# Two layer norms centred by a product into a free bank, token transposes in a second bank, block counting in three pieces, side work at other steps

## The reference, cut to what matters

```python
x = x + gnn0(layernorm(x), adj, ...)                 # stage 1
x = x + experts0(layernorm(x)[None], ...)[0]         # stage 2, 8 experts, top 2
x = x + gnn1(layernorm(x), adj, adj, ...)            # stage 3: signed graph attention, 3 heads, and two GRU cells
x = x + experts1(layernorm(x)[None], ...)[0]         # stage 4

def layernorm(x, eps=1e-5):
    return (x - mean(x)) / sqrt(var(x) + eps)

# stage 4
logits = flat @ router_w.T
probs = softmax(logits)
topk_probs, topk_idx = top_k(probs, 2)
topk_probs = topk_probs / (sum(topk_probs) + 1e-9)
h = silu(flat @ w1[e]) * (flat @ w3[e])              # 8 experts, 341 hidden
out = sum over the two experts of gate * (h @ w2[e])
```

## Time and profile before

| | |
|---|---|
| median of three executions | 514.84 us |
| the profiled execution | 515.35 us |
| its span, first to last instruction | 513.5 us |
| mean granted TensorE clock | 0.946 of full |
| TensorE busy | 439.7 us (86%) |
| VectorE busy | 337.6 us (66%) |
| ScalarE busy | 233.6 us (45%) |
| GpSimd busy | 63.6 us (12%) |
| chain that ended last | PE 47%, DVE 26%, ACT 10%, issue 10%, POOL 3%, DMA 2% |

### The profile page before, as it was taken

The page is one execution under the profiler, slowest core; times in us unless marked ns, Lnnn a source line. Parts: engine busy times, 40 slices in busy tenths (PEclk is TensorE's granted clock), DMA queues, the critical chain, the costliest instruction groups (busy, mean ns, idle before and its releaser), DMA issues.

```text
span 513.5 us, 6127 instructions
## 1 busy us (share of the span) xinstructions
PE 439.7 (86%) x1754; PEld 255.0 (50%) x1756; DVE 337.6 (66%) x731; ACT 233.6 (45%) x377; POOL 63.6 (12%) x112
## 2 busy tenths in 40 slices
PE   4578597978799998998979998999987878889996
PEld 2533353544455664454644343444434446666886
DVE  0997979787637684224574789596766726774573
ACT  4988779586777651204034222222222114743431
POOL 5000000000010000000000000100320321264433
PEclk9579788998979999989999999999999989999999
DMA  8989300000000100000000000170100012013132
GB/s 287 301 253 400 138 0 0 0 1 1 0 3 0 54 2 0 1 0 2 0 2 0 1 0 31 50 235 26 37 22 1 22 47 57 28 34 89 59 107 80
DMA packets 25355, 30.44 MB, mean 59 GB/s; under 512 B 3266, under 2 KB 19855, under 8 KB 25319
## 3 DMA queue, kind: packets, MB, share of 16 engines
q1 hardware_dynamic: 22711, 26.56, 16.0%
q0 software_dynamic: 1568, 2.92, 1.7%
q10 hardware_dynamic: 1040, 0.52, 0.4%
HBM read 19.73 MB, written 10.26 MB: 58 GB/s over the span
## 4 chain that ended last, share of the span: by engine, by line
PE 47%; DVE 26%; ACT 10%; issue 10%; POOL 3%; DMA 2%; SPq 0%; DVEq 0%; POOLq 0%; ACTq 0%
PE bank L1344 8%; PE bank L1162 5%; DVE pr_ring L2120 3%; PE bank L1123 3%; PE bank L1421 3%; PE bank L1405 3%; PE bank L1292 2%; PE bank L1406 2%; DVE y_units L1546 2%; POOL xg L586 2%; DVE y_units L1557 2%; PE bank L1012 2%; PE bank L1333 2%; DVE t_units L1552 2%; DVE hr_ring L1921 2%
## 5 line engine op out<-in xcount | busy, mean ns | idle before, releaser
L1344 PE MATMUL bank<-pr_ring,hW 128*128 128x512 f32 (+3 forms) x198 | 94.5, 562 | 8.2 <-DVE pr_ring L2120 7.3
L2120 DVE SCALAR_TENSOR_TENSOR pr_ring<-adjT,regR,bank 128x512 f32<-128x512 f32 (+3 forms) x99 | 64.3, 680 | 34.4 <-PE bank L1333 33.2
L1344 PEld LDWEIGHTS bank<-pr_ring,hW 128*128 128x128 f32 (+1 forms) x198 | 34.3, 193 | 39.7 <-DVE pr_ring L2120 23.2
L1012 PE MATMUL bank<-y_units,msg 128*128 128x512 f32 (+3 forms) x66 | 34.4, 653 | 14.5 <-DVE y_units L1567 14.5
L1123 PE MATMUL bank<-hr_ring,W2s 128*128 128x512 f32 (+1 forms) x96 | 46.3, 571 | 0.0
L1921 DVE TENSOR_TENSOR hr_ring<-hr_ring,bank 128x512 f32<-128x512 f32 (+1 forms) x48 | 29.5, 621 | 22.5 <-ACT hr_ring L808 16.0
L808 ACT ACTIVATE hr_ring<-bank,b1c 128x512 f32<-128x512 f32 (+1 forms) x48 | 29.7, 628 | 15.5 <-PE bank L985 15.5
L983 PE MATMUL bank<-zhi,W1hi 128*128 128x512 f32 (+1 forms) x48 | 35.8, 747 | 0.3 <-DVE zlo L1541 0.3
L586 POOL DMA_INDIRECT xg<-rowx,slot x22 | 22.1, 1005 | 72.2 <-DVE slot L1678 62.6
L2161 DVE TENSOR_TENSOR hbuf<-hbuf,bank 128x341 f32<-128x341 f32 x30 | 15.3, 508 | 19.9 <-PE bank L1406 17.6
L1012 PEld LDWEIGHTS bank<-y_units,msg 128*128 128x128 f32 (+1 forms) x66 | 14.0, 224 | 27.8 <-DVE y_units L1567 18.3
(11 more groups left out here) (350 smaller groups left out, 871.2 us busy)
## 6 DMA issues: line engine op xcount, KB each, us to landing
xg<-zeros SPq DMA_DIRECT2D x1, 6110.0 KB
wall<-in_w SPq DMA_DIRECT2D x2, 1364.0 KB
adjT<-in_adjT SPq DMA_DIRECT2D x1, 2560.0 KB
xblk<-xg SPq DMA_DIRECT2D x30, 65.0 KB, 1.8
adjT<-in_adjT SPq DMA_DIRECT2D x1, 1650.0 KB
adjT<-in_adjT SPq DMA_DIRECT2D x3, 512.0 KB, 5.7
adjT<-in_adjT SPq DMA_DIRECT2D x1, 1024.0 KB
W1f<-in_W SPq DMA_DIRECT2D x1, 1024.0 KB, 11.6
```

Of the source, the lines that this page charges most:

```text
L1012: mm = nc.tensor.matmul(B_GNN[:, 0:w], msg[0:r, j, :], y_units[0:r, g % RINGY, i, 0:w], start=(j == 0), stop=(j == T - 1))
L1344: nc.tensor.matmul(B_ACC[:, 0:w], hW[0:r, j, k * P:(k + 1) * P], ring[0:r, 0:w], start=(k == 0 and j == 0), stop=(k == K - 1 and j == T - ...
L2120: nc.vector.scalar_tensor_tensor(out=pr_ring[0:r, 4 + p % R_RING, 0:w], in0=adjT[0:r, j, cols(c)], scalar=g_col[0:r, j, k:k + 1], in1=B_F[ ...
```

## The change

The norms of stage 4's chunks 0 and 1 are centred in another way. `mean` becomes a product of cmat (the unit matrix less 1/128) with xT, which gives x less its mean directly, into bk[2], one of the GRU cells' banks. ScalarE squares it from that bank, the first instruction of `scale` reads it there, and VectorE's `center` (line 1520) is gone for these two. The token transposes of chunks 0 and 1 go to bk[1] instead of B_SIDE, and the later gates products that use bk[1] wait for the copy. `starts` is cut in three pieces of 5, 5 and 3 instructions. Some entries of the tables move to other steps. The same number of instructions remains, but for the two centerings.

```diff
 MAIN_PE = {
-    (1, 10): [("mid", 0, 2)], (2, 1): [("turned", 3)], (2, 9): [("turned", 4)], ...
-    (3, 10): [("turned", 6)], (4, 0): [("turned", 7)], (4, 4): [("turned", 8), ("mean", 3, 0)], (4, 7): [("var", 3, 0)], (4, 10): [("logits", 3)],
-    (5, 1): [("ztok", 0)], (5, 3): [("prefix", 0)], (6, 0): [("gates", 1, 1)], (6, 2): [("mid", 1, 1)], (6, 8): [("mean", 3, 1)],
-    (7, 0): [("var", 3, 1)], (7, 4): [("logits", 4)], (7, 5): [("ztok", 1)], (7, 7): [("prefix", 1)]}
+    (1, 10): [("mid", 0, 2)], (2, 3): [("turned", 3)], (2, 9): [("turned", 4)], ...
+    (3, 10): [("turned", 6)], (4, 0): [("turned", 7)], (4, 4): [("turned", 8)], (4, 5): [("mean", 3, 0)], (4, 7): [("var", 3, 0)], (5, 0): [("logits", 3), ("ztok", 0)],
+    (5, 4): [("prefix", 0)], (6, 0): [("gates", 1, 1)], (6, 2): [("mid", 1, 1)], (6, 9): [("mean", 3, 1)],
+    (7, 0): [("var", 3, 1)], (7, 5): [("logits", 4), ("ztok", 1)], (7, 9): [("prefix", 1)]}
 MAIN_DVE = {
-    (0, 0): [("blend", 0, 0)], (0, 4): [("add", 0, 0)], ...
+    (0, 2): [("blend", 0, 0)], (0, 5): [("add", 0, 0)], ...
-    ... (4, 8): [("center", 3, 0)],
-    (5, 0): [("scale", 3, 0)], (5, 3): [("scores", 3), ("ranks", 3), ("picks", 3)], (5, 5): [("weights", 3)], (5, 7): [("slots", 3)],
-    (6, 5): [("mid", 1, 1)], (6, 7): [("blend", 1, 1)], (6, 9): [("add", 1, 1)], (7, 1): [("center", 3, 1)], (7, 5): [("scale", 3, 1)],
-    (7, 8): [("scores", 4), ("ranks", 4), ("picks", 4)], (7, 10): [("weights", 4)], (8, 1): [("slots", 4)], (8, 3): [("starts", 0)], (8, 6): [("list", 0)]}
+    (4, 10): [("scale", 3, 0)], (5, 2): [("scores", 3), ("ranks", 3), ("picks", 3)], (5, 4): [("weights", 3)], (5, 6): [("slots", 3)],
+    (6, 5): [("mid", 1, 1)], (6, 7): [("blend", 1, 1)], (6, 9): [("add", 1, 1)], (7, 4): [("scale", 3, 1)],
+    (7, 7): [("scores", 4), ("ranks", 4), ("picks", 4)], (7, 9): [("weights", 4)], (8, 0): [("slots", 4)], (8, 4): [("starts", 0)], (8, 6): [("starts", 1)],
+    (8, 10): [("starts", 2), ("list", 0)]}
 MAIN_ACT = [
-    ... ("center", 3, 0), ("var", 3, 0), ("rank", 3), ("ztok", 0), ... ("center", 3, 1), ("var", 3, 1), ("rank", 4), ("ztok", 1)]
+    ... ("center", 3, 0), ("var", 3, 0), ("ztok", 0), ("rank", 3), ... ("center", 3, 1), ("var", 3, 1), ("ztok", 1), ("rank", 4)]
+def centred(l, c):
+    return l == 3 and c < C - 1
+        B_XC, B_TOK = bk[2], bk[1]
+        def ln_means(n):
+            return sum(not centred(*key) for key in LN_ORDER[:n + 1])
+        def token_bank(name, c):
+            return B_TOK if (name, c) in (("htok", 0), ("htok", 1)) else B_SIDE
             def ln_square(l, c):
+                if centred(l, c):
+                    xc = B_XC[:, 0:width(c)]
             def tokens(c, name, n):                                    # ScalarE
-                read = B_SIDE[:, 0:k * P].rearrange("p (t d) -> p t d", t=k)
+                read = token_bank(name, n % C)[:, 0:k * P].rearrange("p (t d) -> p t d", t=k)
             def ln_mean(l, c):                                         # TensorE
+                if centred(l, c):
+                    nc.tensor.matmul(B_XC[:, 0:w], cmat[:, :], xT[:, cols(c)], start=True, stop=True).then_inc(s["ln_xc"], 1)
+                    return
             def gates(n, c):                                           # TensorE, second cell
+                    at(pe, "htok_set", C + c)
             def last_gates():
+                at(pe, "htok_set", C + C - 1)
             def tokens(c, name, n, x):                                 # TensorE
-                take_side(f"{name}_set", n + 1)
+                bank = token_bank(name, c)
+                if bank is B_SIDE:
+                    take_side(f"{name}_set", n + 1)
             def ln_center(l, c):                                       # VectorE
-                at(dve, "ln_mean", n + 1)
+                if centred(l, c):
+                    return
+                at(dve, "ln_mean", ln_means(n))
             def ln_scale(l, c):
-                nc.vector.scalar_tensor_tensor(out=xc, in0=xc, scalar=-0.5, in1=y, ...)
+                nc.vector.scalar_tensor_tensor(out=xc, in0=B_XC[:, 0:w] if centred(l, c) else xc, scalar=-0.5, in1=y, ...)
-            def route_starts():
+            def route_starts(part):
```

More of the change, by code:

```diff
@@ L141 @@
     (0, 5): [("spread", 7)], (0, 6): [("spread", 8)], (0, 7): [("turned", 2)], (0, 9): [("mid", 0, 1)], (1, 7): [("gates", 0, 2)],
-    (1, 10): [("mid", 0, 2)], (2, 1): [("turned", 3)], (2, 9): [("turned", 4)], (2, 10): [("turned", 5), ("gates", 1, 0)], (3, 3): [("mid", 1, 0)],
-    (3, 10): [("turned", 6)], (4, 0): [("turned", 7)], (4, 4): [("turned", 8), ("mean", 3, 0)], (4, 7): [("var", 3, 0)], (4, 10): [("logits", 3)],
-    (5, 1): [("ztok", 0)], (5, 3): [("prefix", 0)], (6, 0): [("gates", 1, 1)], (6, 2): [("mid", 1, 1)], (6, 8): [("mean", 3, 1)],
@@ L145 @@
-    (7, 0): [("var", 3, 1)], (7, 4): [("logits", 4)], (7, 5): [("ztok", 1)], (7, 7): [("prefix", 1)]}
+    (1, 10): [("mid", 0, 2)], (2, 3): [("turned", 3)], (2, 9): [("turned", 4)], (2, 10): [("turned", 5), ("gates", 1, 0)], (3, 3): [("mid", 1, 0)],
+    (3, 10): [("turned", 6)], (4, 0): [("turned", 7)], (4, 4): [("turned", 8)], (4, 5): [("mean", 3, 0)], (4, 7): [("var", 3, 0)], (5, 0): [("logits", 3), ("ztok", 0)],
+    (5, 4): [("prefix", 0)], (6, 0): [("gates", 1, 1)], (6, 2): [("mid", 1, 1)], (6, 9): [("mean", 3, 1)],
@@ L146 @@
+    (7, 0): [("var", 3, 1)], (7, 5): [("logits", 4), ("ztok", 1)], (7, 9): [("prefix", 1)]}
 MAIN_DVE = {
-    (0, 0): [("blend", 0, 0)], (0, 4): [("add", 0, 0)], (1, 0): [("mid", 0, 1)], (1, 4): [("blend", 0, 1)], (1, 6): [("add", 0, 1)],
+    (0, 2): [("blend", 0, 0)], (0, 5): [("add", 0, 0)], (1, 0): [("mid", 0, 1)], (1, 4): [("blend", 0, 1)], (1, 6): [("add", 0, 1)],
     (1, 7): [("top", 1)], (2, 0): [("share", 1)], (2, 1): [("rest", 1, 0)], (2, 2): [("rest", 1, 1)], (2, 4): [("mid", 0, 2)],
@@ L149 @@
     (2, 6): [("blend", 0, 2)], (2, 7): [("add", 0, 2)], (2, 10): [("top", 2)], (3, 3): [("share", 2)], (3, 4): [("rest", 2, 0)],
-    (3, 8): [("mid", 1, 0)], (3, 10): [("rest", 2, 1)], (4, 1): [("blend", 1, 0)], (4, 4): [("add", 1, 0)], (4, 8): [("center", 3, 0)],
-    (5, 0): [("scale", 3, 0)], (5, 3): [("scores", 3), ("ranks", 3), ("picks", 3)], (5, 5): [("weights", 3)], (5, 7): [("slots", 3)],
-    (6, 5): [("mid", 1, 1)], (6, 7): [("blend", 1, 1)], (6, 9): [("add", 1, 1)], (7, 1): [("center", 3, 1)], (7, 5): [("scale", 3, 1)],
@@ L153 @@
-    (7, 8): [("scores", 4), ("ranks", 4), ("picks", 4)], (7, 10): [("weights", 4)], (8, 1): [("slots", 4)], (8, 3): [("starts", 0)], (8, 6): [("list", 0)]}
+    (3, 8): [("mid", 1, 0)], (3, 10): [("rest", 2, 1)], (4, 1): [("blend", 1, 0)], (4, 4): [("add", 1, 0)],
+    (4, 10): [("scale", 3, 0)], (5, 2): [("scores", 3), ("ranks", 3), ("picks", 3)], (5, 4): [("weights", 3)], (5, 6): [("slots", 3)],
+    (6, 5): [("mid", 1, 1)], (6, 7): [("blend", 1, 1)], (6, 9): [("add", 1, 1)], (7, 4): [("scale", 3, 1)],
@@ L1526, in ln_scale @@
                 at(dve, "ln_y0", n + 1)
[L1527 removed]
+                nc.vector.scalar_tensor_tensor(out=xc, in0=B_XC[:, 0:w] if centred(l, c) else xc, scalar=-0.5, in1=y, op0=ALU.mult, op1=ALU.mult).then_inc(s["ln_step"], 1)
                 at(dve, "ln_y2", n + 1)
@@ new lines, in route_starts @@
+                if part == 0:
+                    link(nc.vector.tensor_tensor(held, base[0:1, 2, :], base[0:1, 0, :], ALU.subtract))
+                    link(nc.vector.tensor_scalar(full, held, 1.0 / P, 0.5 / P - 0.5, ALU.mult, ALU.add))
+                    whole(full)
+                    link(nc.vector.scalar_tensor_tensor(out=key, in0=full, scalar=-float(P), in1=held, op0=ALU.mult, op1=ALU.add))
+                    link(nc.vector.scalar_tensor_tensor(out=key, in0=key, scalar=float(E), in1=turn_no, op0=ALU.mult, op1=ALU.add))
+                elif part == 1:
+                    link(nc.vector.tensor_tensor(square, key.unsqueeze(1).to_broadcast([1, E, E]), key.unsqueeze(2).to_broadcast([1, E, E]), ALU.is_gt))
+                    link(nc.vector.tensor_reduce(share1, square, AX.X, ALU.add))
+                    link(nc.vector.tensor_reduce(most, full, AX.X, ALU.add))
+                    link(nc.vector.tensor_scalar(share1, share1, most, float(EARLY), ALU.add, ALU.is_lt))
+                    link(nc.vector.tensor_tensor(share1, share1, full, ALU.add))
+                else:
+                    link(nc.vector.tensor_tensor(square, tri[0:1, :, :], share1.unsqueeze(1).to_broadcast([1, E, E]), ALU.mult))
+                    link(nc.vector.tensor_reduce(opens, square, AX.X, ALU.add))
+                    link(nc.vector.tensor_tensor(closes, opens, share1, ALU.add))
@@ L2272, in _ @@
                         if c == 1:
-                            gat_side(("starts", 0))
+                            for part in range(3):
+                                gat_side(("starts", part))
                             gat_side(("list", 0))
```

22 lines of the change are left out of this document (4 added, 18 removed).

## The result

The changed kernel takes 509.37 us (median of 13 executions, 508.21 to 514.14) against 514.84 (13 executions, 512.69 to 518.19). The ratio is 0.9907, interval 0.9885 to 0.993: 3.6 to 5.9 us less. The profiled execution took 511.43 us with a span of 509.7, against 515.35 and 513.5.

The account below looks back on a forecast made before the run. Chunk 1's slots(4) was taken to set block 0, and so the time. Terms 0.9 + 0 + 0.4 + 3.7 + 0 = 5.0 us off the median 514.84 gave 509.8 us; range 507.9 to 513.0.

Parts of the forecast that it names:

- The bound: End of chunk 1's slots(4) sets block 0's transpose, 15.7 us later; the loop's own end is early enough.
- A: Loop's start: blend(0,0) moved from step (0,0) to (0,2), add to (0,5); gain 0.9 us, bounds 0 and 1.27.
- B: turned(3) moved from step (2,1) to (2,3): TensorE's wait only moves to attend (2,8); 0 us, bounds 0 and 1.26.
- C: Chunk 0's norm and routing, with centring product, own bank and moved entries: gain 0.4 us, bounds 0 and 0.9.
- D: Chunk 1's norm and routing, with centring product, own bank and moved entries: gain 3.7 us, some 1.6 from half clock gone.
- with it back the part is worth 2.1: Lower bound for chunk 1's part, forecast at 3.7 us, if the stretch at half clock in its routing returns.
- rival 1: Half clock returns in chunk 1's routing, or C or A gives nothing: 511.4 to 512.7 us; chance 0.25.
- E: Loop's end: starts in three pieces, list at (8,10), moved behind the numerators, early enough for block 0: 0 us.
- block 15 not earlier by what block 0 is: Sign listed as showing the prediction wrong: block 0's gain does not reach block 15.
- 2: More than the sum: chunk 0's waits overlap better, variance's lead survives, first blocks' half clock shortens: 507.9 to 508.7; chance 0.10.
- 3: Nothing arrives at the end: second group's first block depends on something that doesn't move: 514.8 us; chance 0.09.
- 4: Slower: VectorE's order makes the clock fall in chunk 0's routing, +6.5, with half clock in chunk 1 too: 517.9; chance 0.06.

Follow-up runs that it names:

- A and B alone: Kernel before with only blend and add of chunk 0 two and one steps later and turned(3) at step (2,3): 515.18 us, single execution.
- the idle products in chunk 0: Kernel before with blend, add and turned(3) moved, plus three idle products ahead of chunk 0's logits: 511.28 us, single execution.
- chunk 1's part alone: Kernel before with only chunk 1's norm centred by the product, its transposes in the other bank and its table entries moved: 508.95 us, ratio 0.9889.
- whole starts: Changed kernel with starts in one piece at (8,3) and list at (8,6), as before: 510.78 us, single execution.
- filled: Changed kernel with 14 idle products after the last gates, where TensorE otherwise waits for block 0: 508.39 us, ratio 0.9871.
- scale later, whole starts: Changed kernel with scale of chunks 0 and 1 at (5,0) and (7,5), and starts in one piece: 506.49 us, ratio 0.9815.
- without A and B: Changed kernel with blend(0,0), add(0,0) and turned(3) back at their old steps: 512.09 us, single execution.
- tables alone: Changed kernel's tables with the old centring on VectorE and the tokens in the shared bank: 510.03 us, single execution.

## Why the prediction was right, and where not

Forecast 509.8, measured 509.37; the sum of 5.0 stands against 4.64 at the marks, and against 3.6 to 5.9 in the times. That the sum came so close is in part luck: at block 0 the gain was 5.33, 0.3 more than forecast, and 0.7 was lost again behind it by a term that I had put at nothing. All "now" values below are marks or durations of the profile after.

**The bound** held: slots(4) set block 0, 15.70 us later, forecast 15.7.

**A** (0.9): 23.85 - 22.98 = 0.87. **B** (0): 0.97 at attend (2,9), so 0.10 more. The wait moved to steps (2,7) and (2,8), 0.51 and 0.26, and was smaller than the 1.26 removed; I had named (2,8) alone.

What I didn't see is that A and B alone would be worth nothing at the end. The kernel with them alone lost them to a clock fall; in the whole change the clock was full in chunk 0's routing, and they were kept. Each side of this is one profile.

**C** (0.4): 1.38 - 0.97 = 0.41, and 0.43 alone. VectorE's wait 1.50 (forecast 1.5), TensorE's 0.98 (1.1).

**D** (3.7): 5.33 - 1.38 = 3.95, and 3.87 alone. On the axis of the profile after, the forecast's times stand 1.38 - 0.79 = 0.59 earlier. Mean 384.39 (measured 384.38), variance 386.75 (386.75), logits 392.47 (392.60), scores 393.55 (393.59), slots' end 400.31 (400.09): the 0.15 added for hand-overs wasn't needed. Of TensorE's waits in this part, 1.45, 0.4 and 1.3, the middle one doesn't follow from the text: the wait for x of 0.83 less a step of 0.70 is 0.13, and 0.13 was measured.

**The step that was wrong in D** is the bound "with it back the part is worth 2.1", and with it the price of rival 1 (511.4 to 512.7). The 1.6 for the half clock was right in the old order: 1.66 by the idle products in chunk 0. It is not right in the new one: with the half clock back, D alone still brought 3.87. I took what TensorE lost in its own steps, 1.4 and 1.6 us instead of 0.70, for what the path loses, and with the new order and the second bank the path runs over VectorE there. D's 3.95 can be split as about 1.65 from the clock and 2.3 from the centring, the bank and the order (attend (6,8) to slots(4): 21.45 before, 19.80 at full clock in the old kernel's tables, 17.50 after); but D brings nearly the whole even without the clock (3.87). My reason for a full clock, that TensorE stands still less before, is not borne out either: chunk 1's part alone has the same waits as the changed kernel, and its clock fell.

**The step that was wrong in E** is "0 us". The times were right: list_set forecast at 409.8 on this axis, measured 409.76; last gates' end 411.6, measured 411.37. I asked only whether they come too late. They come too early: the loop ends 1.84 us earlier with the pieces, nothing can use it, and TensorE's longer standstill, 3.40 instead of 1.31, puts the first blocks at half clock for longer. Against the kernel before this costs 0.7 (48.45 - 47.78), against the same kernel with whole starts 2.1, and where `scale` is later 0.9. So the gain at block 0, 156.07 - 150.74 = 5.33, is down to 4.66 at block 15 and 4.64 at the end. The prediction's own test ("block 15 not earlier by what block 0 is") shows this.

**The rivals.** 1: the half clock did not come back in chunk 1 in the profiled execution; with the new table entries for chunk 1 it did in two kernels where its price can be read, and that was 0.10 and 0.12 (attend (6,8) to slots(4) 17.60 and 17.62, against 17.50). 2: its times lie within the spread of single executions, but the mechanism it names did not come: the half clock at the blocks grew. 3: out, the end moved. 4: out for the change; its clock fall came in the kernel with A and B alone, and cost 1.2.

**Open.** Why the clock falls in one routing and not in the next is not settled. A part of it can be the execution's and not the kernel's: over its 13 executions the changed kernel's mean granted clock runs from 0.946 to 0.960, and the kernel before's from 0.946 to 0.966 over those run beside the experiments. Only the filled and the unfilled wait of over 3 us stand on several profiles each. The changed kernel and the one with chunk 1's part alone have the same TensorE wait of 1.23 in front of the logits; the clock is 1.00 in the one and 0.50 in the other. When that wait comes may count: it ends at mark 126.0 in three profiles (the changed kernel, whole starts, filled), and the clock stays full; it ends at 127.0 to 127.4 in three others (chunk 1 alone, without A and B, tables alone), and the clock falls in each. No run moves the wait alone. Before the blocks, waits of 1.31 (whole starts) and 1.3 (scale later, whole starts) ended the one at full clock and the other at half. No filled wait was followed by a fall (three kernels). The token bank by itself was not tried.

With the wait filled, 2.14 are gained at block 15 but 1.46 at the end. The lead is whole up to the last block's first product (230.57, changed 232.70) and shrinks behind it. There VectorE makes `joiner`, the last block's table of places, and in this profile the instruction starts 0.05 us after an addition on GpSimd and lasts about as long as that does; `hbuf` of the last block stands behind it. The timelines of VectorE and GpSimd, the filled kernel first and then the changed one:

```profile
493.34 2.35 POOL L633 TENSOR_TENSOR answer<-x3tok,picked_y 128x1024 f32<-128x1024 f32 x1 [1.91 <-DMA picked_y<-yg]
493.39 2.52 DVE L2166 TENSOR_SCALAR joiner<-place_id,own 128x384 f32<-128x384 f32 x1
```
```profile
498.67 0.42 DVE L2165 TENSOR_SCALAR joiner<-place_id,own 128x384 f32<-128x384 f32 x1
499.14 2.35 POOL L633 TENSOR_TENSOR answer<-x3tok,picked_y 128x1024 f32<-128x1024 f32 x1 [2.46 <-DMA picked_y<-yg]
```

It isn't the filling: the last `joiner` took 2.40 to 2.56 in the three profiles where it started behind that addition (one of them, the change without A and B, has nothing filled) and 0.42 in the eleven where it started ahead of it.

## What to carry to other kernels

Price a stretch at half clock by the engine that the path runs over there: a stretch over chunk 1's scores cost 1.66 us where VectorE waited for TensorE and 0.1 where it didn't. Ask of every piece of work made earlier what waits behind it: a TensorE that is done early and stands still in front of a TensorE-bound stage can lose 0.7 to 2.1 us where the earliness brings nothing. In a queue in order, put what must wait behind the work that others wait for (`scale` behind one more numerator: 1.9 us), and compare such kernels at marks behind a common point, since here single executions differ by more than the parts. Don't build on one profile where the clock is concerned: the same blocks took 46.2 to 46.5 us in three profiles with whole starts and 47.7 to 47.8 in five.

## What the hardware showed that I had not expected

- A half-speed TensorE can be free: scores to slots took 6.50 us with the clock at 0.50 over the first half of it and 6.50 at 1.00 throughout.
- With three idle products ahead of chunk 0's logits the clock was full there and also in chunk 1's routing, 40 us later (136.98 against 139.62 at slots(4), of which 0.99 is the lead and 1.65 the clock). The second I can't explain, and one execution doesn't show that the products did it.
- A VectorE instruction that starts behind a GpSimd one can last as long as that: `joiner` took 0.42 us alone and 2.52 us beside GpSimd's addition of 2.35 us.
- An operand from PSUM instead of SBUF cost `scale`'s first instruction nothing (0.69 and 0.69). An estimate from the fixed parts of the Trainium skill (VectorE: DVE Perf Modes, the section on the TRN2 errata), 120 cycles with a PSUM source and 58 from SBUF, is 0.065 us more; for this operand the measurement decides.
